# Second layer's rows transform: pixels of a tile ordered by column, 64x64 blocks of two tiles on four quarters of TensorE

## The reference, cut to what matters

```python
xp = jnp.einsum('bhwc,mc->bhwm', xc, w_pw1)                 # 256 -> 512 channels
xp = star_scale * jnp.square(jax.nn.relu(xp)) + star_bias
xf = jnp.fft.rfft2(xp, axes=(1, 2), norm='ortho')
weight = jnp.einsum('bfc,hwf->bhwc', routeing.astype(cw.dtype), cw)
spatial_weight = jnp.einsum('bfc,hwf->bhwc', spatial_routeing, spatial_weights)
xs = jnp.fft.irfft2(xf * weight, s=(H, W), axes=(1, 2), norm='ortho')
out = xp * spatial_weight + xs
out = jnp.einsum('bhwm,dm->bhwd', out, w_pw2)               # 512 -> 256 channels, added to x
```

## Time and profile before

| | before |
|---|---|
| median of three runs | 759.1 us |
| span of the profiled execution | 758.5 us |
| TensorE busy | 681.3 us (90%) |
| VectorE busy | 557.5 us (73%) |
| GpSimd busy | 342.3 us (45%) |
| ScalarE busy | 329.1 us (43%) |
| mean granted TensorE clock | 0.976 |

### The profile page before, as it was taken

How to read it: one execution, slowest core, us unless ns; L and a number is a source line. 1 busy time by engine, 2 the same in 40 slices (tenths; PEclk the granted TensorE clock), 3 DMA queues, 4 the chain that set the end, 5 groups by cost and what they waited for, 6 DMA issues and landing times.

```text
span 758.5 us, 9182 instructions
## 1 busy us (share of the span) xinstructions
PE 681.3 (90%) x3590; PEld 374.5 (49%) x3590; DVE 557.5 (73%) x656; ACT 329.1 (43%) x488; POOL 342.3 (45%) x200
## 2 busy tenths in 40 slices
PE   3969999889999699997999998999699988988896
PEld 2755767779955464432214564444532334335332
DVE  5997989978669626521543244799999999994698
ACT  4725810010014143122552111689879959743262
POOL 6810039999806322000000002449998969930060
PEclk9989999999999899999998999999989999999999
DMA  5069300674007024626164002000000000000002
GB/s 197 1 93 144 43 0 1 104 114 115 1 1 266 10 102 173 243 85 247 70 207 168 1 0 87 1 1 1 0 2 1 2 0 1 1 1 1 14 1 111
DMA packets 37768, 49.53 MB, mean 65 GB/s; under 512 B 2644, under 2 KB 26004, under 8 KB 36396
## 3 DMA queue, kind: packets, MB, share of 16 engines
q1 hardware_dynamic: 37724, 48.94, 23.8%
HBM read 28.19 MB, written 10.49 MB: 51 GB/s over the span
## 4 chain that ended last, share of the span: by engine, by line
PE 51%; DVE 29%; POOL 8%; ACT 5%; issue 3%; DMA 2%; SPq 0%; DVEq 0%; POOLq 0%
DVE psum L434 13%; PE psum L866 6%; PE psum L938 5%; PE psum L1180 4%; PE psum L1051 4%; PE psum L1152 4%; POOL arena L2194 3%; PE psum L808 3%; PE psum L903 3%; PE psum L1014 2%; PE psum L1036 2%; POOL arena L2208 2%; PE psum L874 2%; PE psum L912 2%; PE psum L955 2%
## 5 line engine op out<-in xcount | busy, mean ns | idle before, releaser
L434 DVE SCALAR_TENSOR_TENSOR psum<-arena,psum 128x1024 f32<-128x1024 f32 x123 | 158.4, 1288 | 3.9
L2283 POOL TENSOR_TENSOR arena<-arena 128x1024 f32<-128x1024 f32 x76 | 151.2, 2025 | 11.4 <-ACT arena L2022 11.1
L866 PE MATMUL psum<-arena 128*128 128x128 f32 x800 | 92.8, 274 | 7.0 <-DVE arena L512 5.8
L2022 ACT ACTIVATE arena<-arena 128x1024 f32<-128x1024 f32 x80 | 92.1, 1184 | 8.3 <-POOL arena L2283 8.2
L512 DVE TENSOR_TENSOR arena<-arena,psum 128x2048 f32<-128x2048 f32 x37 | 82.0, 2280 | 15.6 <-PE psum L866 7.0
L866 PEld LDWEIGHTS psum<-arena 128*128 128x128 f32 x800 | 86.9, 140 | 13.3 <-DVE arena L512 10.7
L1152 PE MATMUL psum<-arena 64*64 64x512 f32 x648 | 79.8, 610 | 2.2 <-ACT arena L2064 1.8
L2242 POOL MEMSET arena<- 128x864 f32 x1 | 0.8, 837 | 173.0 <-DVE arena L1615 173.0
L512 POOL TENSOR_TENSOR arena<-arena 128x2048 f32<-128x2048 f32 x13 | 47.0, 3661 | 1.3 <-PE psum L866 1.2
L1152 PEld LDWEIGHTS psum<-arena 64*64 64x64 f32 x648 | 22.4, 132 | 46.1 <-issue 46.1
L1068 PE MATMUL psum<-arena 128*128 128x512 f32 x96 | 41.5, 593 | 1.0 <-ACT arena L1799 1.0
(11 more groups left out here) (257 smaller groups left out, 1246.3 us busy)
## 6 DMA issues: line engine op xcount, KB each, us to landing
arena<-fc_w_dram SPq DMA_DIRECT2D x10, 1024.0 KB, 9.4
bounce<-arena SPq DMA_DIRECT2D x32, 256.0 KB, 2.0
arena<-bounce SPq DMA_DIRECT2D x32, 256.0 KB, 4.8
arena<-arena SPq DMA_DIRECT2D x16, 480.0 KB
arena<-x_dram SPq DMA_DIRECT2D x4, 512.0 KB, 4.9
out_dram<-arena SPq DMA_DIRECT2D x3, 512.0 KB, 2.6
arena<-sp_w_dram SPq DMA_DIRECT2D x1, 1152.0 KB
arena<-arena SPq DMA_DIRECT2D x8, 140.0 KB
```

The costliest lines, as they stand in the source:

```text
L434: return eng.scalar_tensor_tensor(dst, tap_view(t, a, b), wt, filter_acc, ALU.mult, ALU.add)
L866: m = pe.matmul(psum[:, 4 * hf + xx // 4, xx % 4 * P:(xx % 4 + 1) * P], prods[n % NB][:, xx * P:(xx + 1) * P], ident, start=(first and xx ...
L2022: a.activation(tap_tmp(n).rearrange("p (y x) -> p y x", y=H), tap_view(t, tap, b), ACT.Copy, scale=col("dw2_w", t * K5 + tap)).then_inc(s_ ...
L2283: g.tensor_tensor(dst, dst, tap_tmp(n), ALU.add).then_inc(s_ta, 1)
```

## The change

The pixels of a tile are put in another order, partition 32 i + y in place of 4 y + i. The transform over y then is block diagonal (four blocks of 32x32), so it is done as two 64x64 blocks, and two tiles share one go over the four quarters of the array: quarter (half, to) takes rows `half` of tile `2 pair + to` and writes partitions `to` of PSUM bank `half` of the pair. `U[:, t]` so holds the same half of two tiles, and each is stored by two DMAs. TensorE does a pair at every second step, behind the L903 of that step. `Zc1` is written in the order of the tiles, by reads of X with a step of 32 pixels; `update_x1` reads and writes X with that step too. The spatial weights, the first transform's matrix and the last one's columns are put in order on the host. The counts of the semaphores follow.

```diff
--- before.py
+++ after.py
@@ -279,6 +279,9 @@
         V = [words(o + 4096 * b, 4096).rearrange("p (t c) -> p t c", t=WT) for b in range(B)]; o += 8192
         craw = words(o, 4096)[0:PARTS * NF].rearrange("p (a m) -> p a m", a=4)
         ccoef = words(o + 4096, 2048)[0:PARTS * NF].rearrange("p (a m) -> p a m", a=2)
+
+        def by_column(a):
+            return a.rearrange("p (y i o) -> p o i y", i=4, o=WT)
 
         def by_block(a):
             return a.rearrange("p (t k m) -> p t k m", t=WT, k=2)
@@ -697,9 +700,12 @@
             for b in range(B):
                 for t in range(WT):
                     sp.wait_ge(s_f1e, WT * b + t + 1)
-                    sp.dma_start(w["bounce"][0, b, :, t, :], U[b][:, t, :]).then_inc(s_uo[b], 16)
+                    pair, half = divmod(t, 2)
+                    spectra = w["bounce"][0, b].rearrange("(n i) w c -> w i n c", i=4)
+                    for to in range(2):
+                        sp.dma_start(spectra[2 * pair + to, 2 * half:2 * half + 2], U[b][y_rows(to), t, :]).then_inc(s_uo[b], 16)
             for b in range(B):
-                sp.wait_ge(s_uo[b], 16 * WT)
+                sp.wait_ge(s_uo[b], 32 * WT)
             for c in range(3, NCB):
                 sp.dma_start(chunk_at[c], w["fc2_w"][c]).then_inc(s_str[c], 16)
             for b in range(B):
@@ -717,7 +723,7 @@
                     sp.wait_ge(s_i2e, WT * b + t + 1)
                     rows = w["bounce"][1, b].rearrange("s w c -> (s w) c")[t * P:(t + 1) * P, :]
                     sp.dma_start(rows, U[b][:, t, :]).then_inc(s_uo[b], 16)
-                sp.wait_ge(s_uo[b], 32 * WT)
+                sp.wait_ge(s_uo[b], 48 * WT)
                 for t in range(WT):
                     sp.dma_start(V[b][:, t, :], w["bounce"][1, b, :, t, :]).then_inc(s_vi[WT * b + t], 16)
 
@@ -900,16 +906,20 @@
                         pe.wait_ge(s_pw1r, i - 3)
                     b, t = divmod(i, WT)
                     for k in range(HALVES):
-                        m = pe.matmul(psum[:, i % 4, :], Zc1[:, 2 * k + b, t::WT], pw1w[:, k], start=(k == 0), stop=(k == 1))
+                        m = pe.matmul(psum[:, i % 4, :], Zc1[:, 2 * k + b, t * P:(t + 1) * P], pw1w[:, k], start=(k == 0), stop=(k == 1))
                     m.then_inc(s_pw1, 1)
-                if i >= 3:
-                    n = i - 3
-                    pe.wait_ge(s_xpd, n + 1)
-                    if n < 4:
+                if i >= 4 and i % 2 == 0:
+                    pair = i // 2 - 2
+                    pe.wait_ge(s_xpd, 2 * pair + 2)
+                    if pair < 2:
                         pe.wait_ge(s_cvr, 4)
                     else:
-                        pe.wait_ge(s_f1e, n - 3)
-                    pe.matmul(psum[:, 4 + n % 4, :], dft[:, 0], xp[:, n, :], start=True, stop=True).then_inc(s_f1, 1)
+                        pe.wait_ge(s_f1e, 2 * pair - 2)
+                    for to, half in ((0, 0), (1, 1), (1, 0), (0, 1)):
+                        rows = y_rows(half)
+                        m = pe.matmul(psum[y_rows(to), 4 + 2 * (pair % 2) + half, :], dft[rows, 0, rows], xp[rows, 2 * pair + to, :],
+                                      start=True, stop=True)
+                    m.then_inc(s_f1, 1)
 
             pe.wait_ge(s_w1b, 48)
             pe.wait_ge(s_pw1r, TILES)
@@ -1324,8 +1334,10 @@
                 dve.wait_ge(s_gn_coef, layer + 1)
                 if layer in (1, 2):
                     for i in ((0, 1), (0, 2))[layer - 1]:
-                        v.tensor_scalar((Zc1, Zc2)[layer - 1][:, i], X.rearrange("p h b q -> p (h b) q")[:, i], grs[:, i:i + 1],
-                                        gnb[:, i:i + 1], ALU.mult, ALU.add).then_inc(s_zc, 1)
+                        src, dst = X.rearrange("p h b q -> p (h b) q")[:, i], (Zc1, Zc2)[layer - 1][:, i]
+                        if layer == 1:
+                            src, dst = by_column(src), dst.rearrange("p (o i y) -> p o i y", o=WT, i=4)
+                        v.tensor_scalar(dst, src, grs[:, i:i + 1], gnb[:, i:i + 1], ALU.mult, ALU.add).then_inc(s_zc, 1)
                 if layer == 2:
                     return
                 if layer == 3:
@@ -1611,8 +1623,8 @@
                 for mh in range(HALVES):
                     j = 2 * m + mh
                     dve.wait_ge(s_p2, j + 1)
-                    xv = X[:, mh, b].rearrange("p (j o) -> p o j", o=WT)[:, 4 * q:4 * q + 4, :]
-                    v.tensor_tensor(xv, psum[:, 4 + j % 4, :].rearrange("p (o j) -> p o j", o=4), xv, ALU.add).then_inc(s_x_new, 1)
+                    xv = by_column(X[:, mh, b])[:, 4 * q:4 * q + 4]
+                    v.tensor_tensor(xv, psum[:, 4 + j % 4, :].rearrange("p (o i y) -> p o i y", o=4, i=4), xv, ALU.add).then_inc(s_x_new, 1)
 
             for i in range(TILES):
                 dve.wait_ge(s_sw, i + 1)
@@ -1790,7 +1802,8 @@
                     return
                 if layer == 1:
                     for i in (2, 3):
-                        flatten(zc, i, s_act0)
+                        a.activation(zc[:, i].rearrange("p (o i y) -> p o i y", o=WT, i=4), by_column(X.rearrange("p h b q -> p (h b) q")[:, i]),
+                                     ACT.Identity, scale=grs[:, i:i + 1], bias=gnb[:, i:i + 1]).then_inc(s_act0, 1)
                 if layer == 2:
                     for i in (1, 3):
                         flatten(zc, i, s_zc)
@@ -1956,7 +1969,7 @@
                 if i >= 4:
                     n = i - 4
                     b, t = divmod(n, WT)
-                    act.wait_ge(s_f1, n + 1)
+                    act.wait_ge(s_f1, n // 2 + 1)
                     if n == 0:
                         act.wait_ge(s_cwe, 1)
                     a.activation(U[b][:, t, :], psum[:, 4 + n % 4, :], ACT.Copy).then_inc(s_f1e, 1)
@@ -1995,8 +2008,8 @@
                     b, t = divmod(n, WT)
                     act.wait_ge(s_i2, n + 1)
                     if n == 0:
-                        act.wait_ge(s_uo[0], 16 * WT)
-                        act.wait_ge(s_uo[1], 16 * WT)
+                        act.wait_ge(s_uo[0], 32 * WT)
+                        act.wait_ge(s_uo[1], 32 * WT)
                     a.activation(U[b][:, t, :], psum[:, 6 + n % 2, :], ACT.Copy).then_inc(s_i2e, 1)
                 if i + NS < TILES:
                     copy_spectrum(i + NS)
@@ -2004,7 +2017,7 @@
                 b, t = divmod(n, WT)
                 act.wait_ge(s_o1, n + 1)
                 if t == 0:
-                    act.wait_ge(s_uo[b], 32 * WT)
+                    act.wait_ge(s_uo[b], 48 * WT)
                 a.activation(OT[b][:, :, t, :], psum[:, 2 + n % 2, :].rearrange("p (k j) -> p k j", k=KM), ACT.Copy).then_inc(s_o1e, 1)
 
 
@@ -2346,7 +2359,7 @@
     r["spectra"] = np.tile(r["spectra"], (PARTS, 1, 1))
     r["spectra_coef"] = np.broadcast_to(sign, (PARTS * NF, 2, 1024))
 
-    r["spatial_w"] = i["L1_conv_spatial_weights"].reshape(P, WT, NF).transpose(2, 1, 0).reshape(NF, PIX)
+    r["spatial_w"] = i["L1_conv_spatial_weights"].reshape(H, 4, WT, NF).transpose(3, 2, 1, 0).reshape(NF, PIX)
     r["spatial_w"] = np.tile(r["spatial_w"], (PARTS, 1))
 
     chan = np.concatenate([[24 * (16 * gr + m // 8) + off + m % 8 for m in range(P)]
@@ -2414,7 +2427,9 @@
                     f2s[a, m, q] = e.real if part else -e.imag
     blocks = [[np.linalg.inv(f2[a])[64 * h:64 * h + 64, 64 * h:64 * h + 64].T for h in range(2)] for a in range(2)]
     twice = [np.vstack([np.hstack(pair)] * 2) for pair in blocks]
-    mats = [f1.T, f2[0].T, f2[1].T, f2s[0].T, f2s[1].T, twice[0], twice[1], np.linalg.inv(f1).T]
+    by_column = f1.reshape(H, 4, H, 4).transpose(1, 0, 3, 2).reshape(P, P)
+    back = np.linalg.inv(f1).T.reshape(P, H, 4).transpose(0, 2, 1).reshape(P, P)
+    mats = [by_column.T, f2[0].T, f2[1].T, f2s[0].T, f2s[1].T, twice[0], twice[1], back]
     return np.stack(mats, 1).astype(np.float32)
```

## The result

The changed kernel takes 785.85 us (median of four runs, 784.93 to 787.88) against 759.47 beside it: ratio 1.0341, 95% interval 1.0313 to 1.0369. It is slower by 26 us; 756.1 was forecast, with 753.6 to 758.8 for 8 in 10. Its profiled execution has a span of 783.7 us, 25.2 more than that of before.

A forecast was written before the change was run, and what follows sets the result against it. TensorE alone was taken to bound the loop, VectorE the stage in front. L938 starting 3.8 us earlier, less 0.8 for the clock, gains 3.0: 759.1 - 3.0 = 756.1 us, range 753.6 to 758.8 for 8 in 10.

The forecast's parts named there:

- Transfers: Stores in the loop: 32 half-tile stores instead of 16, 1.0 us of SP issuing per tile, hidden; otherwise 0.5 us.
- The cover: Weight chunks behind the stores go out from 298.94 and are used from 340.93: stores hidden by 40 us.
- Rival 3: After L938: a transfer, the last weight chunks, sets that stage and the gain ends there; 759.1 us, chance 0.07.
- rival 4: TensorE's groups: quarters run one after another; 762.1 us in two turns, 774.1 one by one, chance 0.08.
- the three signs of being wrong: Group over 1.5 us; first group after 262.5; or a stage behind L938 growing by what the loop saves.
- Quarters: Rows transform on TensorE: a pair costs 1.11 us instead of 1.72, saving 0.61, bounds 0.83 and 0.42.
- The lower bound of 0.89 for a group: Rows transform on TensorE: a pair's cost if changing the array's shape has no price.
- The order in the head: Loop's start: L903 of tile 4 fills 1.72 us of TensorE's 5.95 us pause; first group waits for two scaled tiles.
- the term of 0.77: Loop's start: first group needs two scaled tiles rather than one, +0.77 us, bounds 0.7 and 1.5.
- Reads by column: Normalisations reading X by 128-byte steps: first transform starts 0.8 us later, bounds 0 and 2.3; ScalarE's two cost nothing, at most 0.3.
- rival 2: TensorE's head and end pauses: low clock takes the gain back, leaving 1.2 us; 757.9 us, chance 0.18.

The follow-up runs named there:

- rows_outer: Changed kernel with each store's DRAM pattern 32 x 2 x 512 instead of 2 x 32 x 512, through the constants' order; 758.3 us, ratio 0.9959 to the kernel before.

## Why the prediction was wrong

*The step that failed* is "Transfers": that 32 stores of half a tile are hidden because SP can issue two per tile in 1.0 us, priced from the 2.05 us of four issues. It counted issues and bytes, and never the engines that carry them. Those issues were of whole-width patterns, 0.51 us each; the new pattern starts with a dimension of 2, and an issue took 2.44 us in the median. From the first issue at 263.55 to the last landing at 349.95 it was 86.4 us, and TensorE had work until 337.3. Behind that came the chunks' issues and the read back, 13.4 us more, so TensorE waited 26.16. (The read back itself took 11.3 us to land in the median, 4.3 before. It is now issued directly behind the four chunks of 1 MB; that these hold it up is likely and not tested.) The cover was said to be 40 us for the weight chunks; the nearer user, the read back of the same rows, was not named. Rival 3 ("it doesn't arrive") looked at the chunks behind L938 and so had the right kind of place with the wrong cause and no price. No rival had this sign by this way; rival 4, the only slower one, was about TensorE and did not happen. Of the three signs of being wrong the last came: a stage behind L938 grew.
The Trainium skill, DMA: Bandwidth & Descriptors, section Rules for kernel authors, states it: a DMA's number of engines is set by the slowest dimension that isn't 1, so an outermost one of size c under 16 confines it to at most c. The runs agree for 2 and 4: shares of 0.13 and 0.26, rates of 49 and 88 GB/s; with 8 no cap shows at 101 GB/s. The rule and the diff together would have named the two engines ahead of any run, though not the 26 us.

*Quarters.* 1.02 us a group, as priced (1.03). The way back costs more: 3.64 us for two tiles, not 3.44, so 4.66 a pair against 4.55 forecast; the change of shape is 0.16 + 0.20, not 0.17 + 0.08. (The lower bound of 0.89 for a group stands in no row shown there; two passes are 0.86.)

*The order in the head.* As forecast, L909 of tile 4 ran in the pause. The first two scalings took 3.48 us where 2.96 were counted, so the term of 0.77 came out at 1.29, near its upper bound of 1.5. The second scaling took 1.30 us in place of 0.75, and VectorE's square of tile 4 ran beside it, as the bound supposed.

*Reads by column.* A strided L1340 takes 1.18 us undisturbed (a contiguous one 0.81), just under the 1.2 to 1.95 forecast; the pair takes 4.36, the second held up while GpSimd works. VectorE's first square came 1.06 us later, of which 0.28 was there before the normalisation began (233.57 against 233.29), so 0.78 where 0.8 was taken. ScalarE's went from 1.23 to 2.20 us and was hidden: TensorE waited 0.26 us for it, ahead of its pause. L1627 got slightly faster, 1.05 for 1.09. The first group started at 260.88, 0.8 later than forecast: the 0.28 and the 0.5 of the second scaling.

*The clock, and what is left of the gain.* Both pauses were followed by half the clock, the second too, which the forecast had at even chances: 5.82 and 2.68 us of pause, the groups at 1.9 us behind them, and 4.98 for 3.64 on the tiles after the first (2.2 us lost in the head, not 1.91). The forecast put TensorE 3.8 us ahead at L948 with the clock up. In `rows_outer`, where nothing hides it, it was 1.0 us ahead at L948's start and 0.15 at its end, since L948 too began at the low clock, and it was behind at the weights. This is rival 2, "the clock takes it back", more than the forecast. The medians still give a gain of 0.4%, 3.1 us by the ratio, as the 3.0 of the forecast. That agreement is luck as far as the traces tell: from normalisation to end the profile is 3.1 us shorter, but 3.6 come from the stage behind the weights, which ran at a granted clock of 1.00 against 0.90. Whether the medians differ for the same reason is open.

## What to carry to other kernels

Whoever reorders rows on the chip also reorders them in DRAM: write the pattern of each DMA out and look at its first dimension before counting bytes. If it is small (2 cost 26 us here, 4 and 8 nothing that can be told), turn the order of the rows in the constants so that the long dimension comes first, or split the DMA along the short one. Before a transfer is called hidden, find the first instruction that reads its bytes. And before two profiles are compared, look at the stages that the edit left alone: if they differ, the spans do not tell what the edit did.

## What the runs showed of the hardware

A store with 2 outermost carried 48 to 51 GB/s in rows of 2 KB, one with 4 88 GB/s in a loop that moves some 100 otherwise, and SP was held at the issue: 2.44 us in the median for 128 KB and 5.0 for 256 KB. A filler of 5.3 us kept the granted clock at 1.0 through a pause that without it was 5.8 us and ended at 0.5. The same untouched stage took 47.1, 50.7 or 52.3 us at a mean granted clock of 1.00, 0.90 or 0.87. GpSimd's scaling of 128x512 took 0.77 us alone, and 2.19 or 6.97 beside VectorE's column sums. A ScalarE activation of 1024 elements took 2.20 us at a step of 32 elements and 1.23 without one, a VectorE tensor_scalar 1.18 and 0.81.
